# Moving the gate quantisation, the last piece and the queue order between two matmul stages of an attention and FFN kernel

## The reference, cut to what matters

```python
x = x + attention(layernorm(x), ctx)          # 16 x 256 tokens of 512
x = act_qdq(layernorm(x))                     # TOK = 4096 tokens
up   = act_qdq(x @ lpbq_dequant(w_up).T)      # 1536 features
gate = act_qdq(x @ lpbq_dequant(w_gate).T)
sig  = fixed_qdq_u16(sigmoid(gate))
gate = act_qdq(gate * sig)
o    = act_qdq(gate * up)
out  = x_before + o @ lpbq_dequant(w_down).T

def act_qdq(x):                               # one scale for the WHOLE tensor
    scale = maximum(max(abs(x)) / 32767, 1e-12)
    return clip(round(x / scale), -32768, 32767) * scale
```

## Time and profile before

| | |
|---|---|
| median of 3 runs | 1499.49 us (1498.81 to 1502.97) |
| the profiled execution | 1501.97 us |
| its span, first to last instruction | 1500.1 us |
| PE / DVE / ACT busy in the span | 1370.2 / 1180.3 / 967.2 us |
| mean granted TensorE clock | 0.969 |

### The profile page before, as it was taken

The page is one execution under the profiler, slowest core; times in us unless marked ns, Lnnn a source line. Parts: engine busy times, 40 slices in busy tenths (PEclk is TensorE's granted clock), DMA queues, the critical chain, the costliest instruction groups (busy, mean ns, idle before and its releaser), DMA issues.

```text
span 1500.1 us, 24408 instructions
## 1 busy us (share of the span) xinstructions
PE 1370.2 (91%) x9186; PEld 771.5 (51%) x9186; DVE 1180.3 (79%) x1790; ACT 967.2 (64%) x2025; POOL 343.3 (23%) x326
## 2 busy tenths in 40 slices
PE   4899999999999999969999999999999308999999
PEld 4566676666666666634444444444444103444444
DVE  6878888888888888756888987888898899565541
ACT  6988888888888887765322224898887894222210
POOL 0544455544445554430111110000000000000000
PEclk9999999999999999989999999999999758999999
DMA  6111111111111111133533333676788999567732
GB/s 230 47 58 58 64 71 71 58 64 71 72 72 58 58 43 43 36 121 125 176 110 123 129 117 134 242 249 240 249 307 298 376 395 354 183 232 236 238 100 84
DMA packets 101556, 224.74 MB, mean 150 GB/s; under 512 B 8768, under 2 KB 21184, under 8 KB 99776
## 3 DMA queue, kind: packets, MB, share of 16 engines
q1 hardware_dynamic: 100864, 219.00, 41.1%
q10 hardware_dynamic: 576, 4.19, 0.9%
...
## 4 chain that ended last, share of the span: by engine, by line
PE 41%; DVE 6%; issue 5%; ACT 2%; DMA 1%; SPq 0%; POOL 0%; ACTq 0%; POOLq 0%; DVEq 0%
PE ffn_banks L1271 24%; PE ffn_banks L1286 17%; DVE qg L1584 3%; DVE ffn_peaks L1470 1%; ACT qg L1385 1%; DMA ffn_ring<-gates_dram 1%; DVE ffn_rest L1578 1%; DMA ffn_rest<-w_parts_dram 0%; ACT ffn_rest L1333 0%; DVE ffn_wide L1463 0%; ACT qg L1360 0%; ACT ffn_ring L1389 0%; DVE ffn_ring L1560 0%; DVE ffn_rises L1468 0%; ACT ffn_ring L1398 0%
## 5 line engine op out<-in xcount | busy, mean ns | idle before, releaser
L1271 PE MATMUL ffn_banks<-ffn_wide,ffn_rest 128*128 128x512 f16 x2304 | 502.1, 381 | 6.1 <-DVE ffn_wide L1458 2.7
L1271 PEld LDWEIGHTS ffn_banks<-ffn_wide,ffn_rest 128*128 128x128 f16 x2304 | 226.1, 98 | 281.8 <-DMA ffn_rest<-w_parts_dram 5.8
L1286 PE MATMUL ffn_banks<-ffn_rest,ffn_wide 128*128 128x512 f16 x1152 | 251.7, 382 | 70.4 <-DVE ffn_wide L1614 70.4
L1286 PEld LDWEIGHTS ffn_banks<-ffn_rest,ffn_wide 128*128 128x128 f16 x1152 | 113.4, 98 | 208.7 <-issue 74.7
L640 ACT ACTIVATE qg<-score_banks,neg_max 128x128 f32<-128x128 f32 (+1 forms) x512 | 208.2, 450 | 18.8 <-DVE neg_max L512 18.8
L1423 ACT ACTIVATE ffn_u_steps<-ffn_ring,ffn_scales 128x1024 int16<-128x1024 f32 x48 | 55.0, 1148 | 156.9 <-DMA ffn_ring<-ups_dram 136.3
L417 POOL TENSOR_TENSOR qg<-qg,per_sum 128x512 f32<-128x512 f32 x64 | 85.9, 1342 | 267.1 <-DVE per_sum L516 267.1
L1333 ACT ACTIVATE ffn_rest<-ffn_banks,ffn_row_back 128x1024 f32<-128x1024 f32 x66 | 73.0, 1106 | 99.3 <-PE ffn_banks L1271 95.7
L419 POOL TENSOR_TENSOR qg<-qg,per_sum 128x1024 f32<-128x1024 f32 x64 | 133.7, 2088 | 0.0
L640 ACT ACTIVATION_READ_ACCUMULATOR qg<-score_banks,neg_max 128x1 f32 x512 | 121.1, 237 | 0.0
L649 ACT ACTIVATE pt<-ring_banks 128x512 f32<-128x512 f32 x128 | 70.3, 610 | 41.7 <-PE ring_banks L776 40.8
...
## 6 DMA issues: line engine op xcount, KB each, us to landing
ffn_ring<-ups_dram SPq DMA_DIRECT2D x44, 512.0 KB, 5.9
ups_dram<-ffn_rest SPq DMA_DIRECT2D x42, 512.0 KB, 3.3
...
gates_dram<-ffn_rest SPq DMA_DIRECT2D x24, 512.0 KB, 2.6
ffn_ring<-gates_dram SPq DMA_DIRECT2D x24, 512.0 KB, 4.6
signs_dram<-qg SPq DMA_DIRECT2D x24, 512.0 KB, 4.1
...
```

The costliest lines, as they stand in the source:

```text
L1271: last = pe.matmul(banks[:, pair_of(s), half, :], w[:, m % 2, wp, c, :], xq[:, xp, n, c, :], start=(k == 0), stop=(k == 3 * DC - 1))
L1286: last = pe.matmul(down_banks[:, g % 2, t, :], oq[:, g % 2, op, m, t * P:(t + 1) * P], w_down[:, wp, wk, c], start=(start and k == 0), sto ...
```

## The change: what it does

1. T1 goes from 28 to 27: the first parts of the 48 gate pieces lie in slots 0 to 26, the second parts in slots 27 to 46, and slot 47 has no gate work.
2. The last up piece is taken out of PSUM in two halves of 512 columns, the first as soon as its own twelve matmuls are done (`half_filled`, `evacuate_last`), and its peak is taken in halves (`peak_of_last`). The peak of the ups is now closed after all the second parts (`join(3, ...)` behind them). The first unit of the gap is rounded and multiplied in halves.
3. `load_w` is issued at the end of a row's last slot, behind `store_piece` and ahead of that slot's second parts, where it stood at the start of the next slot.
4. The signed stores of the last four doubles and the two ring loads move into the slots, behind the second parts that they wait for.
5. `sizes` comes two slots after the second part instead of three, and all but three of them are done in the slots. Of the five that stood in or right before the gap's loop, three are left: 21 before it, 22 behind unit index 3, 23 behind unit index 8.
6. `unit_order` is another: the kept doubles 21, 22 and 23 are at index 4, 5 and 10 (7, 10 and 13 before), and the two ring units, (5,) and (7,), at index 6 and 7 (4 and 5 before).

```diff
-    T1, T2 = 28, 20
+    T1, T2 = 27, 20
...
-        unit_order = [(16,), (18,), (1,), (3,), (5,), (7,), (9,), (21,), (11,), (13,), (22,), (0, 1), (0, 0), (23,), (4, 0),
...
+        unit_order = [(16,), (18,), (1,), (3,), (21,), (22,), (5,), (7,), (9,), (11,), (23,), (13,), (0, 1), (4, 1), (0, 2),
...
+        late_sizes = {3: 22, 8: 23}
...
-            if c % 2:
-                size_slots[t + 3 if t + 3 < NP - 1 else NP].append(c // 2)
+            if c % 2 and c // 2 < ND - 3:
+                size_slots[t + 2].append(c // 2)
...
-                if t % PIECES == 0 and s // PIECES + 1 < 2 * IC:
-                    load_w(s // PIECES + 1)
+                if t == 0:
+                    load_w(IC + 1)
...
+                if t % PIECES == PIECES - 1 and s // PIECES + 2 < 2 * IC:
+                    load_w(s // PIECES + 2)
...
-                    if c % 2 and c + 8 < NP:
-                        fetch(c + 8)
+                    if c % 2:
+                        if c + 8 < NP:
+                            fetch(c + 8)
                         store_signed(c // 2)
+                    if c in (NP - 3, NP - 1):
+                        load_again(4 + c // 2 - (ND - 2))
...
+            def evacuate_last(s):
+                for half, ready in enumerate((half_filled, filled)):
+                    act.wait_ge(ready, (1, s + 1)[half])
+                    part = act.activation(stage_of(s)[:, half * N:(half + 1) * N], banks[:, pair_of(s), half, :], ACT.Copy,
+                                          scale=row_back[:, 2 * IC - 1:2 * IC])
+                    part.then_inc((act_half, staged)[half], 1)
...
-                    dve.wait_ge(peaked, 2 * NP)
-                    gather(3, peaks[:, NP:2 * NP])
+                    dve.wait_ge(peaked, 2 * NP + 1)
+                    join(3, peaks[:, NP:2 * NP + 1])
+                    quantum(dve, link, sc, "u")
```

62 lines of the change are left out of this document (41 added, 21 removed).

## The result

The changed kernel took 1490.67 us, the median of 5 runs (1489.64 to 1493.25); the kernel before, beside it, 1498.81 (1494.54 to 1502.97). The ratio is 0.9951, with a 95% interval from 0.9933 to 0.9968: faster by 3.3 to 6.7 per mille. The forecast was 1488.5, with a range of 1485.0 to 1495.0. The profiled execution took 1493.25 us, its span 1491.5.

A forecast was written before the change was run, and what follows sets the result against it. PE's pace through 48 slots, the closing of the ups' peak and DVE's 24 units were taken as the bound; 4.3 + 0.4 + 6.3 = 11.0 us off 1501.97 gave 1491.0, as median 1488.5, range 1485.0 to 1495.0.

The forecast's parts named there:

- the three places: PE in the up stage, end of the slots, gap's loop: 4.3, 0.4 and 6.3 us saved, 11.0 in all.
- the shift to the median: From profiled execution to median time: before's median is 2.5 us below its profile, so 1491.0 becomes 1488.5.
- First parts: Gate pieces in 27 slots of the up stage: second parts begin at 1074.4, 4.1 us sooner.
- 13.0 x 3/4: ACT's standing in the first parts, about 13.0 us, falls to 9.8 as late gate loads go from four places to three.
- The weight load: Last row's up weights: issued at 1133.0, landing at 1138.1, 1.3 us to spare; PE's 4.27 us loss goes.
- The reordering by itself just pays for the shift of the slots: Weight load on SP: the new place keeps 28 pieces and 12 peaks ahead; only the 4.1 us earlier start helps.
- The end of the slots: From last up piece to first products: unit index 1 at 1178.9, 4.7 us sooner, 4.27 of them PE's.
- The loop: DVE's products in the gap: standing falls from 7.5 to 1.2 us, 0.9 and 0.3 behind the two late sizes.
- DMA: Loads in the gap: 19.4 MB take 50 us at 388 GB/s, so the last lands with 6 us to spare.
- rival C: Gap's loop: unit loads below 350 GB/s set the pace, 3 to 4 us late, 1492.5 us; chance 0.11.
- B: Up stage: second parts don't begin sooner, weights late again, only the loop's 6.3 us and little more left, 1492.5; chance 0.15.
- D: Second parts: sizes two slots behind make ACT wait for signed stores; slower, 1512 us if landing takes 11; chance 0.03.

The follow-up runs named there:

- c_before: The kernel before, unchanged, measured and profiled once more as a control: 1499.3 us, ratio 0.9997 to the kernel before.
- c_after: The changed kernel, unchanged, measured and profiled once more: 1488.4 us, ratio 0.9939 to the kernel before.
- g1: The changed kernel with gate loads of odd pieces, from the fifth on, issued one slot sooner: 1490.1 us, ratio 0.9945 to the kernel before.
- a2_after: The changed kernel, unchanged, measured again on the chip of a later block: 1493.0 us, ratio 0.9955 to the kernel before.
- n1: The changed kernel with kept doubles at indices 3, 7 and 12 and late sizes behind 6 and 11: 1491.2 us, ratio 0.9951 to the kernel before.
- u4: The changed kernel with the old unit order and the old places of the sizes: 1495.6 us, ratio 0.9967 to the kernel before.
- t28_19: The changed kernel with first parts in 28 slots and second parts in 19: 1493.8 us, ratio 0.9968 to the kernel before.
- u5: The changed kernel with old unit order, old sizes, and last four signed stores and ring loads behind the slots: 1500.2 us, ratio 1.0002 to the kernel before.

## Why the prediction was right, point by point

**Its mechanism and its sum.** In the two profiles, from slot 0 to down, 318.0 became 306.6: 11.4 us, forecast 11.0. By the prediction's own terms it is 4.3 us on PE (forecast 4.3), 1.7 at the end of the slots (0.4) and 5.4 in the loop (6.3): the three places were right, and two errors of opposite sign nearly cancel, which is luck. The medians moved by less: 8.1 us in the first pair, 9.8 and 6.8 in the later blocks. The step that was mis-sized is the base: the 11.0 us were counted from one execution that had the longest gate waits of all the profiles (10.8 us), and with it the late weights and the loss of clock. From c_before to c_after the same three terms are 0.5, 1.3 and 5.8, together 7.6 us. Over all the profiles of the two unchanged kernels, two of the old and three of the new, slot 0 to down is 316.0 and 307.1 on average, 8.9 us. Median less profile was 2.5 for before and 2.6 for after, but for different reasons: before's profiled execution was long in this stretch, after's in the one ahead of slot 0. That the shift to the median came out right is luck too.

**First parts.** Forecast: the first peak beside the second parts 4.1 us sooner, measured 5.8 (151.4 to 145.6 after slot 0). The places that the prediction named are right. All four executions with 28 slots have four waits of 1.9 to 3.5 us, at pieces 7, 19, 31 and 43; all nine with 27 slots and the gate loads in their old place have three of 1.8 to 3.1 us, at 9, 25 and 41. What "13.0 x 3/4" got wrong is that it scaled all of the standing. Of before's 13.0 us only 10.8 were waits for gate loads (of after's 8.1, 6.0), and ACT also waits elsewhere, for up to 1.3 us in all with 28 slots and up to 2.5 with 27, in short waits that come and go between executions. Together the gate waits are 8.4 to 10.8 us with 28 slots and 6.0 to 9.3 with 27. The first second part comes at 142.4 to 142.9 plus these waits with 28 slots and at 141.4 to 141.8 plus them with 27, so the slot itself gives 1.0 us. On average the second parts begin 2.4 us sooner (151.9 to 149.6). g1 takes the waits away.

**The weight load.** "The reordering by itself just pays for the shift of the slots": right. From the first second part to the load's issue it is 56.4 us in both executions of the old kernel and 56.9 in the three of the new one; without the reordering 63.7. The load is wanted at about 212.3 and landed 4.4 to 5.9 us after its issue where PE waited for it. With 5 us, a first second part later than about 150.4 makes it late: so it is in a2_after, n1 and u4 (1.13, 1.35 and 0.89 us), not in after and c_after. Forecast in the profile after: issue 205.9, measured 204.3; last piece 243.4, as forecast.

**The end of the slots.** Forecast index 1 at 251.8, measured 250.5; the second parts ended 1.1 us sooner than forecast (243.6, not 244.8), which is most of it. The half peaks took 0.59 (forecast 0.6). Double 21's size ahead of the loop, of which up to 1 us was said to show, shows 1.4 us in t28_19 and 0.1 or nothing in the three executions of the kernel after.

**The loop.** Forecast 1.2 us of standing left of 7.5; 2.1, 1.4 and 1.2 measured. Named were 0.9 at index 4 (1.5, 1.2 and 1.0 measured) and 0.3 at index 9 (0.2); not named was the load of index 3, 0.90 us late for ACT in after, of which DVE lost 0.4. Undone in turn, the order gives 0.3 to 1.2 and the sizes 1.8. Another 3.3 lie between u4 (4.2) and before (7.5), and the two traces tell where. The fourth size, behind index 12, is in the loop of before only: 0.8 us. The other 2.5 stand at indices 5 and 6, where ACT waited for loads in before (ACT of the kernel before):

```profile
1192.77 2.00 ACT L1412 ACTIVATE ffn_wide<-ffn_ring,ffn_scales 128x2048 int16<-128x2048 f32 x1 [1.73 <-DMA ffn_ring<-ups_dram]
1196.90 2.00 ACT L1412 ACTIVATE ffn_u_steps<-ffn_wide,ffn_scales 128x2048 int16<-128x2048 f32 x1 [2.12 <-DMA ffn_wide<-ups_dram]
```

The ring loads are issued earlier now: the first one left 5.8 us ahead of index 1 before (1177.79 to 1183.60) and 10.7 after (1170.75 to 1181.47). SP of the kernel before:

```profile
1177.79 0.86 SPq L1131 DMA_DIRECT2D ffn_ring<-ups_dram  x1
```

That the earlier issue is what removed these 2.5 us is by subtraction, not shown; the run that was to show it (u5) showed something else.

**DMA and rival C.** The forecast gave the last load 6 us to spare. In the trace ACT waited for it (ACT of the kernel after):

```profile
1229.01 2.00 ACT L1433 ACTIVATE ffn_wide<-ffn_wide,ffn_scales 128x2048 int16<-128x2048 f32 x1 [0.56 <-DMA ffn_wide<-ups_dram]
```

So nothing was to spare on ACT, and only the 1.2 us by which it still ended ahead of DVE (1231.0 to 1232.19) hid this. "ACT's rounding waits for loads anywhere in the gap" was the prediction's sign that C holds. The sign appeared, and C as it was priced, 3 to 4 us, didn't: of the 2.8 us of waits DVE lost 0.4. The load landed 54.6 us behind the last up matmul, not 50. The stretch up to there and, from SP, the first loads for the down stage (after):

```profile
1174.40:1229.00 54.60, 0.00 (x0) 0.00 (x0) 50.37 (x52) 50.77 (x28) 0.35 (x1) 0.52 1.03 401
```
```profile
1216.82 0.37 SPq L1145 DMA_DIRECT2D qg<-signs_dram  x1
1217.24 1.89 SPq L1215 DMA_DIRECT2D ffn_rest<-w_parts_dram  x4
```

The rate was higher than the 388 GB/s of the forecast. The step that failed is the count of bytes: 401 GB/s over 54.6 us are 21.9 MB, not 19.4. Two things were left out of the 17 loads and 1.6 MB of stores: the unit load that ACT issues behind the last piece (1.05 MB), and the loads for the down stage, twelve of 256 KB issued between 1216.82 and 1229, while up loads were still on their way (the last was issued at 1211.4 and landed 17.6 us later). With the engines at a share of 1.03 an earlier issue would hardly have helped; this, and how much each of the two costs, no run tested.

The engines carried 397 GB/s over the gap, so a limit of 358 (the Trainium skill, DMA: Bandwidth & Descriptors, Specifications) is not seen here either. The prediction worked out 54 us from that limit; that the load landed after 54.6 is a coincidence, since the rate was 401 GB/s.

**The other rivals.** B, that the second parts don't begin sooner, is partly true in a2_after and n1 (first second part at 150.7 and 150.9, where after has 147.4 and before 153.2), and down then starts 1.7 to 2.5 us later than in after. D, sizes two slots behind: ACT waited for signed stores for 5.9 us in after, 9.0 in c_after and 12.3 in a2_after, never over 2.6 at once. The second parts took 96.2, 95.5 and 95.6 us there, so these waits cost DVE nothing.
